# Audio tower on one core: the long filter's matrices in 128-column bands, and two VectorE steps in another place

## The chip, the core and the metric

One Trainium2 chip, one of its cores. The metric is the time of one execution on the device in microseconds; "before" is the median of three runs. The profile is of one further execution.

## What is computed

The input is 32 sequences of 750 x 256 in float32. Of each, every second token of three 256-token segments is kept: 3 blocks of 128 tokens. The reference then is, cut to what matters:

```python
h = tok(x)                                 # softmax attention inside each block of 128
h = h + attn(layernorm(h))                 # below
h = h + ffn(layernorm(h))                  # 6 experts, the best 2 of each token weighted
# attn:
q, k, v = (silu(causal_dwconv(x @ W, w4)) for each of Wq, Wk, Wv)
beta = sigmoid(x @ Wb)
delta_out = delta_rule(q, k, v, beta)      # chunked, carries a state over the blocks
fir_short = causal_dwconv(v, fir_short_w)  # 3 taps
fir_long  = causal_dwconv(v, fir_long_w)   # 63 taps, own taps for each of 256 channels
w = softmax(mlp([x, stats of the four branches]) / temp)   # per head
o = w0 * fir_short + w1 * fir_long + w2 * delta_out + w3 * v
return (rmsnorm(o) * o_norm_w) @ Wo
```

The long filter is done as matrix products. For a channel with taps f, a matrix with T[p, j] = f[62 - (j - p)] (non-zero only for j - p from 0 to 62) takes the 128 tokens p of a block to outputs j of the same block (j < 128) and of the next one (j from 128 to 189). Rows p below 64 end at column 125, so they reach no output of the next block.

## The kernel before

The kernel has three stages, each a block of hand-written queues: what an engine does, and when, is the order of the code of that engine, and engines meet through semaphores only. SyncE (SP) issues most DMAs, ScalarE (ACT) the stores of the filtered rows, GpSimd (POOL) the loads and stores of the triangular systems.

**First stage** (`first_phase`): for each of 32 sequences the block attention, the norm, the projections, the short convolutions and what the delta rule needs; results are packed and stored to DRAM (`packa`, `packb`, `systems`), and v is kept on chip in `v_all` (128 tokens x 256 channels x 96 columns, a column a block of a sequence). Beside this SP writes the matrices of the long filter: for each row p of 128 one DMA (`expand`, line 349) copies 190 consecutive taps of each of 256 channels, shifted by p, from `taps` to `toeplitz` in DRAM. 4 rows go out with each sequence.

**Middle stage** (`second_phase`): the long filter on TensorE, in 32 groups (`it`) of 8 channels (`CG`). SP loads a group's matrices into one of four buffers `toep` (`NT = 4`, line 1040); the load of group `it` waits until group `it - 4` has been multiplied (`fl_ready`). For every 4 channels (half a group) TensorE does four main products (line 1073: 128 rows, 128 output tokens, 96 columns) and four spill products (line 1077: what runs over into the next block; 62 output tokens, 64 columns), all float32, each of which the trace shows as two passes. ScalarE copies each half group from PSUM (line 1089). Ten, then three times six passes of a wide product with the identity (`dense`, line 1057) stand at the head of the stage and ahead of groups 8, 16 and 24; their results are not used. VectorE meanwhile solves triangular systems, SP loads the last stage's weights between the bands.

**Last stage** (`third_phase`): a loop of 35 steps, each of which works on four sequences at once: `n = i` in the delta rule, `it = i - 1` in the gate and the mixture, `e = i - 2` in the output projection, the routing and experts 0 to 2, `f = i - 3` in experts 2 to 5. The names that matter here, all on VectorE unless said:

- `delta_out(n, s, b)` (line 1983): scales block b's output from bank 1 into `DL`. TensorE's `q_state(b + 1)` (line 1543) writes bank 1 next and waits for it (`d_ready`).
- `remainder(n, b)` (line 1966): `R` = `VB` - bank 0. TensorE's `updates(b)` (line 1555) reads `R` (`r_copied`).
- `state(n, b)` (lines 1975, 1977): the state from bank 2 into `S`.
- `gate_weights(it)` (lines 2009 to 2013): the four branch weights `WT`. GpSimd's `weigh_fir` and `weigh_v` (lines 2273, 2278) wait for them, and multiply 768 columns each.
- `routing_weights(e)` (lines 2095, 2097, 2099, 2101): the two kept routes' weights `we`; 2095 and 2101 multiply two SBUF tensors of 18 columns.
- `weigh(it, s, r)` (lines 2019, 2022): `DL` or the filtered rows times `WT`, 768 columns.
- `add_expert(e, k, b)` (line 2111): adds expert k's output of block b from PSUM. TensorE's `expert_out` (line 1672) of the same bank waits for it (`acc_done`); `expert_out(e, 0, 2)` waits for `add_expert(f, 5, 2)`.
- `mix_add` (line 2028): sums the branches.

## Time and profile before

| | us |
|---|---|
| median of 3 runs | 2378.38 (2372.26 to 2381.79) |
| the profiled execution | 2393.8 |
| its span, first to last instruction | 2392.1 |
| first stage, to about | 656 |
| middle stage | 656 to 812 |
| last stage | 817 to 2392 |
| TensorE busy | 2251.9 (94%) |
| VectorE busy | 1852.8 (77%) |
| ScalarE busy | 1290.8 (54%) |
| GpSimd busy | 555.5 (23%) |
| moved by DMA | 334.44 MB |

A busy TensorE is not one at its peak: the ends of its instructions are modelled and its clock can be granted at 1.0 (2.4 GHz) or 0.5 (1.2 GHz) of full speed, which the profile gives for every stretch. A DMA share is the mean busy share of 16 DMA engines; it can read a little above 1.

### The profile page before, as it was taken

What the parts mean: (1) busy time and instruction counts of PE and PEld (TensorE: products, weight loads), DVE (VectorE), ACT (ScalarE), POOL (GpSimd) and SP (SyncE); (2) the same over time, 40 slices, a digit from 0 to 9 for tenths busy, and PEclk for the clock granted to TensorE, in tenths of its full rate; (3) what the DMA queues carried; (4) which work ended last, traced back from release to release, by engine and by line L of the source; (5) the groups of instructions that cost most, each with busy time, mean ns of one, the idle gap of its engine ahead of it and who ended that gap; (6) DMA issues with size and microseconds to landing.
All of it is one profiled execution on the core that took longest, in us unless ns stands there. A gap on an engine that the chain in (4) does not pass through costs nothing.

```text
span 2392.1 us, 53303 instructions
## 1 busy us (share of the span) xinstructions
PE 2251.9 (94%) x20796; PEld 1635.1 (68%) x20796; DVE 1852.8 (77%) x5111; ACT 1290.8 (54%) x2632; POOL 555.5 (23%) x413
## 2 busy tenths in 40 slices
PE   5999999999799779999999999999999999999997
PEld 4666666666587666777677767776776677767765
DVE  4999999999868367677778777777777667767765
ACT  4888888888624334544454455445544544454452
POOL 1444444444400011121112111111111121112111
PEclk9999999999958879999999999999999999999999
DMA  3776777777778912233224222322233224222300
GB/s 98 231 245 229 229 241 245 236 238 236 247 241 314 378 60 71 71 108 96 78 70 139 91 77 71 125 81 74 70 132 105 71 70 133 77 71 76 125 21 21
DMA packets 224297, 334.44 MB, mean 140 GB/s; under 512 B 113870, under 2 KB 190766, under 8 KB 215342
## 3 DMA queue, kind: packets, MB, share of 16 engines
q1 hardware_dynamic: 219726, 309.01, 39.1%
q10 hardware_dynamic: 2304, 12.58, 1.3%
q0 software_dynamic: 2016, 9.44, 1.0%
q8 instruction: 165, 2.70, 0.5%
q14 instruction: 86, 0.70, 0.1%
HBM read 191.66 MB, written 164.23 MB: 149 GB/s over the span
## 4 chain that ended last, share of the span: by engine, by line
PE 49%; DVE 7%; ACT 6%; issue 4%; POOL 0%; DVEq 0%
PE bank L1662 7%; PE bank L1672 7%; PE bank L1595 6%; PE bank L1475 4%; PE bank L1555 4%; PE bank L1632 4%; PE bank L1571 2%; PE bank L1507 2%; PE bank L1543 2%; ACT L1808 2%; ACT L1803 2%; DVE v_all L2111 1%; PE bank L1503 1%; PE bank L1485 1%; DVE DL L2019 1%
## 5 line engine op out<-in xcount | busy, mean ns | idle before, releaser
L2111 DVE SCALAR_TENSOR_TENSOR v_all<-bank,we,v_all 128x256 f32<-128x256 f32 x576 | 264.9, 476 | 219.3 <-PE bank L1672 214.3
L739 DVE SCALAR_TENSOR_TENSOR Y<-bank,convw,Y 128x383 f32<-128x383 f32 (+2 forms) x576 | 330.6, 602 | 3.2 <-ACT Y L627 2.9
L1672 PE MATMUL bank<-w2e,HE 128*128 128x256 f32 x1152 | 327.9, 395 | 2.4 <-DVE v_all L2111 2.3
L1662 PE MATMUL bank<-v_all,w1e 128*128 128x384 f32 x768 | 289.6, 500 | 2.4 <-ACT HE L1808 2.3
L445 PE MATMUL bank<-pb,wqkv 128*128 128x384 f32 x768 | 282.4, 491 | 1.8 <-DVE Y L739 1.8
L1672 PEld LDWEIGHTS bank<-w2e,HE 128*128 128x128 f32 x1152 | 198.0, 191 | 55.3 <-issue 19.3
L1808 ACT ACTIVATE HE<-bank 128x384 f32<-128x384 f32 x192 | 94.1, 490 | 248.9 <-PE bank L1662 248.2
L1595 PE MATMUL bank<-v_all,w1g 128*128 128x384 f32 x512 | 193.4, 500 | 2.0
L1662 PEld LDWEIGHTS bank<-v_all,w1e 128*128 128x128 f32 x768 | 134.5, 191 | 75.9 <-issue 19.8
L445 PEld LDWEIGHTS bank<-pb,wqkv 128*128 128x128 f32 x768 | 132.1, 191 | 61.1 <-DVE Y L739 8.3
L1786 ACT ACTIVATE first_stage<-bank 32x384 f32<-32x384 f32 (+1 forms) x192 | 92.2, 480 | 135.7 <-PE bank L1583 119.2
L2273 POOL TENSOR_TENSOR v_all<-v_all,WT 128x768 f32<-128x768 f32 x32 | 48.6, 1518 | 418.0 <-DVE WT L2013 418.0
L627 ACT ACTIVATE Y<-bank,convw 128x384 f32<-128x384 f32 x192 | 114.0, 594 | 46.6 <-PE bank L445 46.6
L2283 POOL TENSOR_TENSOR m<-m,minus_half_q 128x12 f32<-128x12 f32 x32 | 72.6, 2268 | 282.2 <-DVE m L2034 282.2
L1475 PE MATMUL bank<-v_all 64*128 64x256 f32 x768 | 114.4, 418 | 12.7 <-PEq L1030 5.9
L1595 PEld LDWEIGHTS bank<-v_all,w1g 128*128 128x128 f32 x512 | 89.7, 190 | 51.9 <-ACT v_all L1803 14.0
L1786 ACT ACTIVATE W<-bank 128x256 f32<-128x256 f32 x96 | 36.9, 384 | 150.2 <-PE bank L1555 150.2
L2267 POOL TENSOR_TENSOR VB<-v_all 128x768 f32<-128x768 f32 x32 | 47.1, 1472 | 279.8 <-DVE v_all L2062 212.5
L1950 DVE BATCH_NORM_STATS2 ST<-v_all 128x6 f32<-128x128 f32 x384 | 102.3, 282 | 7.7 <-DMA first_stage<-fl 7.7
L2259 POOL TENSOR_TENSOR b<-b,minus_half_q 128x3 f32<-128x3 f32 x32 | 27.1, 848 | 335.0 <-DVE b L2058 335.0
L1475 PEld LDWEIGHTS bank<-v_all 64*128 64x128 f32 x768 | 69.2, 194 | 50.0 <-issue 36.6
L1939 DVE TENSOR_TENSOR v_all<-bank,upper 128x256 f32<-128x256 f32 x192 | 74.4, 416 | 34.6 <-PE bank L1475 34.6
(217 smaller groups left out, 5199.1 us busy)
## 6 DMA issues: line engine op xcount, KB each, us to landing
packa<-pa SPq DMA_DIRECT2D x32, 1932.0 KB, 6.2
v_all<-packa SPq DMA_DIRECT2D x32, 1932.0 KB, 8.1
packb<-pb SPq DMA_DIRECT2D x32, 768.0 KB, 6.1
v_all<-packb SPq DMA_DIRECT2D x32, 768.0 KB, 10.8
toeplitz<-taps SPq DMA_DIRECT2D x128, 190.0 KB, 5.3
toep<-toeplitz SPq DMA_DIRECT2D x32, 760.0 KB, 7.6
packb<-fsk SPq DMA_DIRECT2D x32, 384.0 KB, 2.7
first_stage<-fl SPq DMA_DIRECT2D x32, 384.0 KB, 8.7
```

Of the source, the lines that this page charges most:

```text
L445: mm = pe.matmul(proj_bank[j][:, 0:T], wqkv[:, a, j * P:(j + 1) * P], xnT[:, a, :], start=(a == 0), stop=(a == HALF - 1), skip_group_check ...
L627: act.activation(Y[:, j, :], proj_bank[j][:, 0:T], ACT.Copy, scale=convw[:, j, CK - 1:CK])\
L739: dve.scalar_tensor_tensor(out=Y[:, j, lag:T], in0=proj_bank[j][:, 0:T - lag], scalar=convw[:, j, CK - 1 - lag:CK - lag], in1=Y[:, j, lag: ...
L1475: mm = pe.matmul(bank[odd][:, hh * 2 * P:(hh + 1) * 2 * P], kT[rows, hh, pair * P:(pair + 1) * P], qkb[rows, :, hh, pair * P:(pair + 1) * ...
L1555: mm = pe.matmul(bank[2][:, (h + 1 - wide) * DH:(h + 1) * DH], UF[s][:, even_heads_first(b, h), :], right.unsqueeze(1).broadcast_to([P, wi ...
L1595: pe.matmul(mlp_bank[m][:, 0:T], w1g[:, a, m * P:(m + 1) * P], chans(pb[s], PX)[:, a, :], start=(a == 0), stop=False, skip_group_check=True)
L1662: mm = pe.matmul(bank[6][:, 0:T], w1e[:, a, k, :], YT[s][:, a, :], start=(a == 0), stop=(a == HALF - 1))
L1672: pe.matmul(expert_bank(b), HE[k % 2][:, b * P:(b + 1) * P], w2e[:, k, :], start=True, stop=True)\
L1786: return act.activation(dst, src, ACT.Copy)
L1808: act.activation(HE[k % 2][:, :], bank[6][:, 0:T], ACT.Gelu_apprx_tanh).then_inc(he_ready.sem, 1)
L1950: return dve.bn_stats(ST[:, r, j, :], values[:, 2 * j:2 * j + 2, :].rearrange("p m d -> p d m"))
L2111: dve.scalar_tensor_tensor(out=HA[s][:, b, :], in0=expert_bank(b), scalar=we[s][:, b, k:k + 1], in1=HA[s][:, b, :], op0=ALU.mult, op1=ALU. ...
```

## The change

1. `toeplitz` in DRAM has 128 columns for each row and channel (`BAND`) where it had 190. A row p from 64 up starts 64 columns later, so that its band holds columns 64 to 191 of the matrix.
2. A buffer `toep` has 192 columns a channel (`TW`). A group is loaded by two DMAs: rows 0 to 63 into columns 0 to 127, rows 64 to 127 into columns 64 to 191. The pieces are 512 bytes.
3. The corners that no load writes and the main product reads (rows from 64, columns 0 to 63) are cleared once by VectorE, which TensorE waits for once (`toep_cleared`).
4. The spill product reads rows 64 to 127 only, and has 64 output tokens.
5. In the last stage `delta_out(n, 0)` stands ahead of `routing_weights`, `remainder(n, 1)` ahead of `weigh(it, 2)`, and `remainder(n, 2)` ahead of `add_expert(e, 1, 0)` and `(e, 1, 1)`. Nothing else moves there.

```diff
-TW = P + FL - 1
+BAND = P
+TW = DH + BAND
...
-                        sp.dma_start(dram["toeplitz"][p], dram["taps"][:, bass.ds(P - 1 - p, TW)]).then_inc(expanded, 16)
+                        sp.dma_start(dram["toeplitz"][p], dram["taps"][:, bass.ds(P - 1 - p + p // DH * DH, BAND)])\
+                            .then_inc(expanded, 16)
...
-                    sp.dma_start(toep[it % NT][:, :, :], dram["toeplitz"][:, it * CG:(it + 1) * CG, :])\
-                        .then_inc(toep_loaded[it % NT].sem, 16)
+                    for k in range(P // DH):
+                        rows = slice(k * DH, (k + 1) * DH)
+                        sp.dma_start(toep[it % NT][rows, :, k * DH:k * DH + BAND],
+                                     dram["toeplitz"][rows, it * CG:(it + 1) * CG, :]).then_inc(toep_loaded[it % NT].sem, 16)
...
                 dense(5)
+                pe.wait_ge(tail["toep_cleared"], NT)
...
-                                mm = pe.matmul(acc[0:TW - P, o + NB:o + BLK * NB], toep[s][:, ch, P:],
-                                               v_all[:, it * CG + ch, 0:(BLK - 1) * NB],
+                                mm = pe.matmul(acc[0:TW - P, o + NB:o + BLK * NB], toep[s][DH:P, ch, P:],
+                                               v_all[DH:P, it * CG + ch, 0:(BLK - 1) * NB],
...
+                for s in range(NT):
+                    dve.memset(toep[s][DH:P, :, 0:DH], 0.0).then_inc(tail["toep_cleared"], 1)
...
                         gate_weights(it)
+                    if 0 <= n < NB:
+                        delta_out(n, n % 2, 0)
                     if 0 <= e < NB:
                         routing_weights(e, e % 2)
+                    if 0 <= n < NB:
+                        remainder(n, 1)
                     if 0 <= it < NB:
                         weigh(it, it % 2, 2)
-                    if 0 <= n < NB:
-                        delta_out(n, n % 2, 0)
-                        remainder(n, 1)
...
+                    if 0 <= n < NB:
+                        remainder(n, 2)
                     if 0 <= e < NB:
                         add_expert(e, 1, 0)
                         add_expert(e, 1, 1)
                     if 0 <= n < NB:
-                        remainder(n, 2)
                         delta_out(n, n % 2, 1)
```

Where the instructions stand. First VectorE in the middle of a step of the last stage, from the end of `gate_weights` on; before:

```order
L2013 TENSOR_TENSOR WT<-WT,m 128x48
L2095 TENSOR_TENSOR e<-e 128x18
L2097 TENSOR_REDUCE g<-e 128x3
L2099 RECIPROCAL g<-g 128x3
L2101 TENSOR_TENSOR we<-e,g 128x18
L2019 TENSOR_TENSOR DL<-DL,WT 128x768
L1983 TENSOR_TENSOR DL<-bank,v_all 128x256
L1966 TENSOR_TENSOR R<-VB,bank 128x256
L2111 SCALAR_TENSOR_TENSOR v_all<-bank,we,v_all 128x256
```

And changed (the lines of this part of the file are 8 further down):

```order
L2021 TENSOR_TENSOR WT<-WT,m 128x48
L1991 TENSOR_TENSOR DL<-bank,v_all 128x256
L2103 TENSOR_TENSOR e<-e 128x18
L2105 TENSOR_REDUCE g<-e 128x3
L2107 RECIPROCAL g<-g 128x3
L2109 TENSOR_TENSOR we<-e,g 128x18
L1974 TENSOR_TENSOR R<-VB,bank 128x256
L2027 TENSOR_TENSOR DL<-DL,WT 128x768
L2119 SCALAR_TENSOR_TENSOR v_all<-bank,we,v_all 128x256
```

`delta_out` (1983, now 1991) passed five instructions, `remainder` (1966, now 1974) one.

Second, VectorE later in the same step, around `remainder(n, 2)`; before:

```order
L2028 TENSOR_TENSOR DL<-DL,v_all 128x768 x2
L2111 SCALAR_TENSOR_TENSOR v_all<-bank,we,v_all 128x256 x2
L1966 TENSOR_TENSOR R<-VB,bank 128x256
L1983 TENSOR_TENSOR DL<-bank,v_all 128x256
L2111 SCALAR_TENSOR_TENSOR v_all<-bank,we,v_all 128x256
```

And changed:

```order
L2036 TENSOR_TENSOR DL<-DL,v_all 128x768 x2
L1974 TENSOR_TENSOR R<-VB,bank 128x256
L2119 SCALAR_TENSOR_TENSOR v_all<-bank,we,v_all 128x256 x2
L1991 TENSOR_TENSOR DL<-bank,v_all 128x256
L2119 SCALAR_TENSOR_TENSOR v_all<-bank,we,v_all 128x256
```

`remainder` passed two expert additions.

Third, SP's queue at the head of the middle stage (`toep` loads, and weights of the last stage between them); before:

```order
L1040 DMA toep<-toeplitz 128x1520 x6
L974 DMA itemp<-in_L_attn_gate_log_temp_dram 128x4
L975 DMA rclip<-in_L_ffn_routing_temp_dram 128x1
L1040 DMA toep<-toeplitz 128x1520
L971 DMA onw<-in_L_attn_o_norm_w_dram 64x1 x2
```

And changed:

```order
L1045 DMA toep<-toeplitz 64x8x128 x12
L977 DMA itemp<-in_L_attn_gate_log_temp_dram 128x4
L978 DMA rclip<-in_L_ffn_routing_temp_dram 128x1
L1045 DMA toep<-toeplitz 64x8x128 x2
L974 DMA onw<-in_L_attn_o_norm_w_dram 64x1 x2
```

Each load of 128 rows of 1520 elements became two of 64 rows of 8 pieces of 128 elements; the order is the same.

## Rows read from the trace of the kernel before

**Rows 1.** Windows by stage: us, busy us (instructions) per engine, clock, DMA share, GB/s

```profile
60.00:640.00 580.00, 542.80 (x6413) 389.15 (x6411) 573.48 (x1505) 478.55 (x1051) 263.46 (x213) 1.00 0.73 236
664.00:812.00 148.00, 141.91 (x1042) 123.24 (x1042) 110.42 (x169) 57.85 (x72) 6.14 (x12) 0.78 0.83 304
900.00:2300.00 1400.00, 1374.97 (x11941) 984.67 (x11940) 1027.28 (x3044) 666.10 (x1332) 244.06 (x147) 1.00 0.27 89
```

**Rows 2.** Waits of TensorE, 900 to 2300 us: total us, times, longest

```profile
PE bank L1543 <- DVE DL L1983: 12.4, 29, 0.5
PE bank L1555 <- DVE R L1966: 8.9, 29, 0.3
```

**Rows 3.** Windows of 5 us in the middle stage, columns as in rows 1

```profile
675.00:680.00 5.00, 5.00 (x29) 4.54 (x29) 4.66 (x11) 1.18 (x2) 0.00 (x0) 0.50 0.51 156
...
735.00:740.00 5.00, 0.78 (x4) 0.78 (x4) 4.80 (x6) 0.25 (x1) 0.00 (x0) 0.73 1.02 420
...
785.00:790.00 5.00, 5.00 (x50) 4.52 (x49) 4.83 (x6) 1.73 (x3) 0.00 (x0) 1.00 1.03 423
```

**Rows 4.** Timeline, TensorE, middle stage: start us, us, instruction, [idle before]

```profile
663.87 1.13 PE L1073 MATMUL bank<-v_all,toep 128*128 128x96 f32 x8 [2.19 <-DMA toep<-toeplitz]
...
677.41 2.02 PE L1073 MATMUL bank<-v_all,toep 128*128 128x96 f32 x8
...
680.40 2.02 PE L1073 MATMUL bank<-v_all,toep 128*128 128x96 f32 x8
...
720.91 1.13 PE L1073 MATMUL bank<-v_all,toep 128*128 128x96 f32 x8
...
722.57 1.13 PE L1073 MATMUL bank<-v_all,toep 128*128 128x96 f32 x8
```

**Rows 5.** Waits, 655 to 830 us; the load of line 1040 issued at 724.3 us

```profile
PE bank L1073 <- DMA toep<-toeplitz: 8.1, 4, 4.8
...
DMA to landing us min/median/max: 14.9/14.9/14.9
```

**Rows 6.** Windows with inputs (1 KB), solved systems (128 B), filtered rows (768 B)

```profile
63.00:64.00 1.00, 1.00 (x5) 0.52 (x4) 1.00 (x3) 1.00 (x4) 0.00 (x0) 1.00 0.93 372
...
830.50:831.00 0.50, 0.50 (x39) 0.50 (x36) 0.00 (x0) 0.00 (x0) 0.00 (x0) 0.50 1.23 151
...
834.00:834.50 0.50, 0.50 (x7) 0.50 (x6) 0.00 (x0) 0.00 (x0) 0.00 (x0) 0.50 1.14 376
```

**Rows 7.** Timeline, one step of the last stage: start us, us, instruction, [idle before]

```profile
1541.28 0.17 DVE L2095 TENSOR_TENSOR e<-e 128x18 f32<-128x18 f32 x1
1541.45 1.50 POOL L2273 TENSOR_TENSOR v_all<-v_all,WT 128x768 f32<-128x768 f32 x1 [12.52 <-DVE WT L2013]
...
1541.91 1.07 DVE L2101 TENSOR_TENSOR we<-e,g 128x18 f32<-128x18 f32 x1
1542.90 0.95 DVE L2019 TENSOR_TENSOR DL<-DL,WT 128x768 f32<-128x768 f32 x1
1542.90 1.03 PE L1672 MATMUL bank<-w2e,HE 128*128 128x256 f32 x4
...
1543.88 0.42 DVE L1983 TENSOR_TENSOR DL<-bank,v_all 128x256 f32<-128x256 f32 x1
...
1544.36 0.71 PE L1543 MATMUL bank<-first_stage,v_all 128*128 128x128 f32 x4 [0.43 <-DVE DL L1983]
1544.55 0.48 DVE L2111 SCALAR_TENSOR_TENSOR v_all<-bank,we,v_all 128x256 f32<-128x256 f32 x1
...
1544.90 1.00 PE L1555 MATMUL bank<-R,first_stage 128*128 128x128 f32 x8
...
1545.74 0.65 PE L1672 MATMUL bank<-w2e,HE 128*128 128x256 f32 x2
...
1550.60 1.46 PE L1662 MATMUL bank<-v_all,w1e 128*128 128x384 f32 x4
...
1552.36 0.82 PE L1555 MATMUL bank<-R,first_stage 128*128 128x128 f32 x5 [0.30 <-DVE R L1966]
```

More of the change, by code:

```diff
@@ L101, in audio_tower @@
             "taps": nc.dram_tensor("taps", [D, 512], F32, kind="Internal").ap(),
-            "toeplitz": nc.dram_tensor("toeplitz", [P, D, TW], F32, kind="Internal").ap(),
+            "toeplitz": nc.dram_tensor("toeplitz", [P, D, BAND], F32, kind="Internal").ap(),
         }
@@ L942, in kept_semaphores @@
                   late_stored=sem("late_stored"), fl_stored=[sem(f"fl_stored{g}") for g in range(NH)],
-                  toep_loaded=[Signal(sem(f"toep_loaded{s}"), 16, primed=0) for s in range(NT)],
+                  toep_cleared=sem("toep_cleared"),
+                  toep_loaded=[Signal(sem(f"toep_loaded{s}"), 16 * P // DH, primed=0) for s in range(NT)],
                   fl_ready=Signal(sem("fl_ready"), 2, primed=0), fl_copied=Signal(sem("fl_copied"), 2, primed=0))
```

## The prediction

> **What bounds the kernel now.** I read first the busy time by stage [rows 1], to see which engine each stage has no slack on. In the first stage VectorE is busy 573.48 of 580 us and the DMA engines 0.73 of the time: VectorE bounds it. In the last stage TensorE is busy 1374.97 of 1400 us and VectorE 1027.28: TensorE bounds it, and what it can lose or win is its waits. The middle stage has TensorE busy 141.91 of 148 us, but at a mean granted clock of 0.78, so "busy" hides a slow clock.
>
> Then the waits of TensorE in the last stage [rows 2]: two places carry nearly all of its idle time, line 1543 behind `delta_out` (12.4 us, 29 times) and line 1555 behind `remainder` (8.9 us, 29 times). These are the two steps that the change moves.
>
> Then the middle stage in slices [rows 3] and as a timeline [rows 4]. At 675 to 680 us TensorE is 100% busy at clock 0.50 (1.2 GHz) with the DMA engines 0.51 busy; at 785 to 790 it is as busy at 1.00 (2.4 GHz) with the DMA engines 1.03 busy. In the timeline half a group (4 channels) takes 2.99 us at the low clock (677.41 to 680.40) and 1.66 us at the high one (720.91 to 722.57), so a group costs 5.99 or 3.31 us. The clock is low after two idle stretches: 2.19 us before the first band lands at 663.87 and the starved slice 735 to 740 (TensorE busy 0.78 of 5 us). The load issued at 724.3 landed 14.9 us later, and the longest of TensorE's waits for a load was 4.8 us, of 8.1 in all [rows 5]; with four buffers and 3.31 us a group, a load has 13.2 us. So this stage is bound by DMA landings and by what the clock does behind them.
>
> **The change, part by part.**
>
> *Building the bands (first stage).* 128 DMAs write 128 columns for each of 256 channels, where they wrote 190. Nothing computes with them in this stage and VectorE is what bounds it [rows 1], so I cost it at nothing. The cover is large: a third fewer bytes cannot make it later.
>
> *Clearing the corners.* Four VectorE memsets of 64 rows x 512 elements stand at the head of the middle stage, in front of VectorE's wait for the first stage's stores. TensorE waits for them once, behind ten dense matmuls, after which it sits idle 2.19 us for the first band anyway [rows 4]. Nothing, unless the four took longer than those matmuls and that idle together; the 768-column multiply takes 0.95 us [rows 7], so four of 512 columns are under 4.
>
> *The second matmul of each channel.* It reads 64 rows and 64 columns for 128 rows and 62. In half a group eight main passes take 1.13 us of 1.66 [rows 4], so eight spill passes take about 0.6 us; two columns more in 62 is 3% of that at the most, 0.02 us x 64 halves = 1.2 us. I take nothing for it.
>
> *The loads.* A group was one DMA of 128 rows of 6080 bytes; now it is two DMAs of 64 rows, each row 8 pieces of 512 bytes (1024 pieces, 64 for each of 16 DMA engines, against 8 rows each). What an engine needs for a piece has to come from neighbours. At 785 to 790 us the DMA engines move 423 GB/s at a share of 1.03 [rows 3], nearly all in rows of 4 KB and more: 25.7 GB/s an engine, so 6080 bytes take 237 ns and a group 8 x 237 = 1.90 us. No row has 512-byte pieces into SBUF. Pieces of 1 KB (the inputs) move 372 GB/s at 0.93, 41 ns each; of 768 bytes (the filtered rows) 376 at 1.14, 37 ns; of 128 bytes (the solved systems) 151 at 1.23, 17 ns [rows 6]. The straight line from 128 to 768 bytes gives 29 ns at 512, so 64 x 29 = 1.86 us a group. The bounds are 20 ns (512 bytes at 25.7 GB/s), 1.28 us, and 37 ns (a piece costs what a 768-byte one does), 2.37 us. I take 29 ns, which lies between two measured neighbours: **a third fewer bytes, but the same DMA time**. So the late landing near 739 us stays late, the two low-clock stretches stay, and the stage gives 0 us, with -0.6 to +0.5 us a group as its bounds.
>
> *The first moved step (last stage).* Rows 7 show one step. `delta_out(0)` (line 1983) ends at 1544.30 and line 1543 starts at 1544.36; TensorE's line 1672 before it (4 passes, from 1542.90, 0.217 us apart) would have let it start at 1543.77, so this wait costs 0.59 us. The order now is `delta_out(0)`, four small routing operations, `remainder(1)`, the 0.95 us `weigh`. `delta_out(0)` reads PSUM and ends at about 1541.75: line 1543 starts at 1543.77. But look at GpSimd. Its multiply of 1.50 us begins at 1541.45, and line 2101, a VectorE multiply of two SBUF tensors with 18 columns, takes 1.07 us and ends as that multiply ends; its sister line 2095, issued 0.17 us before GpSimd starts, takes 0.17. Behind `delta_out(0)` line 2095 is issued at about 1541.65, inside GpSimd's multiply, and waits until 1542.95; GpSimd's second multiply, of the same size, then begins, and line 2101, ready at 1543.6, waits until about 1544.5. `remainder(1)` ends at about 1544.85, line 1555 starts at 1544.90 as before, and the 0.59 us is given back. Worse, `weigh` and then the expert addition end at 1546.1 where it was 1545.03; line 1672, which starts at 1545.74 and needs it, now starts 0.42 us late.
>
> The Trainium skill (SBUF — State Buffer, Who interferes with whom) states this as a rule: a VectorE instruction with two SBUF inputs and a GpSimd instruction that reads SBUF exclude each other, and the second to issue blocks for the whole of the first. The trace agrees at line 2101 (1.07 us for 0.17). Without such an exclusion the first move would be worth its 0.59 us.
>
> *The second moved step.* `remainder(2)` comes ahead of two expert additions. Line 1662 (4 passes of 0.486 us from 1550.60, 0.325 apart) would let line 1555 start at 1551.89; it starts at 1552.36, 0.47 us late. The two additions that now stand behind it take 0.48 us each, more than the wait, so the wait goes. They end 0.4 us later; line 1672 that needs them stands behind eight passes of line 1555 and four of 1543. Late next is `delta_out(1)`, by my count 0.1 us ahead of its reader.
>
> **Sum.** A step: +0.42 - 0.47 = -0.05 us, x 30 steps = -1.5 us; middle 0; first 0. The profiled execution took 2393.8 us (span 2392.1), 15 us above the median of 2378.38, so I subtract from the median: **2377 us**. About 0.5%, 12 us, is what a measurement of this kernel tells from no change.
>
> **Rivals.**
>
> 1. *The exclusion does not bite* (GpSimd starts later, or line 2095 slips in front). Then both waits go, 0.59 + 0.47 = 1.06 us x 30 = -32 us: 2346 us. For it: both waits are real [rows 2]. Against it: line 2101.
>
> 2. *The bands land sooner.* At 20 ns a piece, the five groups queued before 739 us land 3 us sooner; the 4.8 us wait shrinks to under 2, shorter than the 2.19 us after which the clock fell, and two groups at 3.31 instead of 5.99 us give 5 more. If the first band also comes in time for TensorE to stay at 2.4 GHz, the eight groups before the first dense block between groups give 8 x 2.68 = 21 us. So -10 to -30 us: 2358 us. Against it: 768-byte pieces are already slower per byte than 1 KB ones [rows 6].
>
> 3. *Slower: the half-height loads starve TensorE.* If 64 rows take in only half the full rate (411/2 = 205 GB/s), each half of a group (262 KB) takes 1.28 us, a group 2.56, +0.66 us. It decides wherever the DMA engines have no slack: five groups before 739 us (+3 us) and the last 16 groups (785 to 790 us: share 1.03), +11 us; where a wait then drops the clock, each group costs 2.68 us more. +14 us, up to +35: 2392 us. No row shows a 64-row load of any size, so nothing here excludes it. The Trainium skill (SBUF — State Buffer, Door 1) says that partitions 0 to 63 reach 8 of 16 DMA ports and that two loads on the two halves serialize. By its 218 GB/s a group would take 2.4 us (an estimate from that page). Against it: stores on ScalarE's queue fill the gaps.
>
> 4. *The late expert addition costs more than the second move returns*: 0.42 us a step without the 0.47 is +13 us, 2391 us.
>
> **How the numbers follow.** Forecast (within 12 us) 0.41; rival 1 0.14, rival 2 0.17; rival 3 0.21, rival 4 0.07. So faster 0.31, same 0.41, slower 0.28. The forecast's own range is 2366 to 2388. Rival 1 at its full size sets the low end, 2346; rival 3 with some clock loss sets the high end, 2400; its +35 us is left out.
>
> **What would show it.** Right: the granted clock still 0.50 for the first eight groups, with a DMA share of about 0.5; a load near 724 us landing after some 15 us; the first routing multiply (line 2103 of the changed kernel) taking about 1.3 us and the last (2109) about 1.0, with no wait at line 1543 for b = 1 and a new wait of about 0.4 us at line 1672 behind the expert addition; steps as long as now. Wrong: both routing multiplies at 0.17 us (rival 1), the middle stage shorter than 140 us (rival 2), or TensorE waits on the band loads well over 8.1 us and a DMA share near 1 with fewer GB/s (rival 3).

## The result, and the profile after

| | before | changed |
|---|---|---|
| median, us | 2377.81 (4 runs) | 2403.91 (4 runs) |
| lowest to highest | 2372.26 to 2381.79 | 2400.04 to 2414.30 |
| ratio | | 1.012 (1.0094 to 1.0146) |
| the profiled execution | 2393.8 | 2400.7 |

The change makes the kernel 1.2% slower, +26 us, where 2377 was forecast. The two profiled executions lie only 7 us apart: the profile of before is of one of its longer executions (2393.8 us against a median of 2377.81), as the experiments below show.

The stages first, windows of the changed kernel (columns as in rows 1):

```profile
60.00:640.00 580.00, 543.12 (x6450) 389.40 (x6449) 573.64 (x1506) 478.44 (x1052) 264.21 (x214) 1.00 0.65 223
664.00:812.00 148.00, 139.94 (x936) 120.49 (x935) 110.41 (x169) 52.25 (x65) 5.94 (x11) 0.71 0.92 225
900.00:2300.00 1400.00, 1376.34 (x11905) 997.73 (x11905) 1057.96 (x3053) 664.78 (x1330) 223.40 (x148) 1.00 0.28 91
```

Against [rows 1]: the first stage is as it was, with less DMA (share 0.65 for 0.73). The middle stage has 936 matmul passes in the same 148 us for 1042, at a clock of 0.71 for 0.78; the DMA engines are busier (0.92 for 0.83) and move less (225 GB/s for 304). That is the reading that decides: the DMA engines are nearly full through the whole stage and do less.

The head of the middle stage, 5 us windows of the changed kernel; beside them [rows 3] and, at 660 to 670, 403 and 413 GB/s before:

```profile
660.00:665.00 5.00, 2.47 (x15) 1.41 (x14) 0.55 (x12) 0.00 (x0) 1.84 (x3) 1.00 1.03 206
665.00:670.00 5.00, 5.00 (x33) 4.47 (x31) 0.00 (x0) 1.64 (x2) 0.00 (x0) 0.58 1.11 253
670.00:675.00 5.00, 4.07 (x25) 3.60 (x24) 0.00 (x0) 1.64 (x2) 0.00 (x0) 0.50 1.12 257
675.00:680.00 5.00, 4.71 (x24) 4.42 (x24) 3.93 (x11) 0.83 (x1) 0.00 (x0) 0.50 1.23 199
```

A share over 1 with 199 to 257 GB/s: all engines are occupied and move 49 to 62% of what they did at the head before (403 and 413 GB/s). From 670 us on TensorE is not full even at 1.2 GHz. Its waits in this stage, 655 to 830 us:

```profile
PE bank L1079 <- DMA toep<-toeplitz: 10.6, 6, 4.7
```

That is 10.6 us for 8.1 in [rows 5], little beside the 12 us by which the two profiles differ in this stage; a list of waits doesn't show the time that a busy TensorE spends at 1.2 GHz. Whether the clock is the cause or only follows the late loads, this profile can't tell; the run with fourteen dense passes below can.

How long one packet takes is read from the DMA summary of 660 to 680 us (20 us of 16 engines, 320 us in all), the load queue's row; first before, then changed:

```profile
q1 hardware_dynamic: 1359, 4.69, 61.6%
```
```profile
q1 hardware_dynamic: 6053, 2.98, 83.2%
```

Changed: 0.832 x 320 / 6053 = 44 ns a packet, nearly all of them the 512-byte pieces. A group is 0.524 MB: 266.2 us / 2.98 MB x 0.524 / 16 = 2.93 us of all engines. Before it was 197.1 / 4.69 x 0.778 / 16 = 2.04 us. (The share is the packets' time as the profile counts it, so these figures serve to compare kernels in the same window and no more.) The prediction had 29 ns and 1.86 us.

The last stage, one step of the changed kernel, timeline (columns as in rows 7):

```profile
1552.79 0.42 DVE L1991 TENSOR_TENSOR DL<-bank,v_all 128x256 f32<-128x256 f32 x1
1552.84 1.50 POOL L2283 TENSOR_TENSOR v_all<-v_all,WT 128x768 f32<-128x768 f32 x1 [12.50 <-DVE WT L2021]
...
1553.13 1.24 DVE L2103 TENSOR_TENSOR e<-e 128x18 f32<-128x18 f32 x1
...
1554.30 1.50 POOL L2288 TENSOR_TENSOR v_all<-v_all,WT 128x768 f32<-128x768 f32 x1
...
1554.82 1.00 DVE L2109 TENSOR_TENSOR we<-e,g 128x18 f32<-128x18 f32 x1
1555.16 0.61 PE L1551 MATMUL bank<-first_stage,v_all 128*128 128x128 f32 x4
1555.75 0.41 DVE L1974 TENSOR_TENSOR R<-VB,bank 128x256 f32<-128x256 f32 x1
...
1556.21 1.10 PE L1563 MATMUL bank<-R,first_stage 128*128 128x128 f32 x8 [0.44 <-DVE R L1974]
1556.95 0.47 DVE L2119 SCALAR_TENSOR_TENSOR v_all<-bank,we,v_all 128x256 f32<-128x256 f32 x1
...
1557.47 0.70 PE L1680 MATMUL bank<-w2e,HE 128*128 128x256 f32 x2 [0.16 <-DVE v_all L2119]
...
1563.67 1.00 PE L1563 MATMUL bank<-R,first_stage 128*128 128x128 f32 x8
```

This is the predicted step nearly to the number: 2103 held until GpSimd's first multiply is done (1.24 us), 2109 until its second is (1.00), line 1551 without a wait, `remainder(1)` late again (0.44 us at line 1563), a new wait at line 1680, and the second `remainder` in time. TensorE's waits, 900 to 2300 us:

```profile
PE bank L1563 <- DVE R L1974: 14.7, 30, 1.8
PE bank L1680 <- DVE v_all L2119: 4.5, 28, 0.2
```

19.2 us for the 21.3 of [rows 2].

### The profile page after: what moved, and what is told of

It reads as the page before. It is cut to its first block, busy times and chain, and to the rows that moved or that the text cites. A ratio compares the mean times of both kernels' runs of the same rounds, so it can differ in the third digit from the quotient of the medians.

```text
span 2399.0 us, 53340 instructions
## 1 busy us (share of the span) xinstructions
PE 2257.6 (94%) x20796; PEld 1650.2 (69%) x20796; DVE 1880.5 (78%) x5115; ACT 1289.0 (54%) x2632; POOL 531.4 (22%) x413
## 4 chain that ended last, share of the span: by engine, by line
PE 57%; ACT 6%; DVE 4%; DMA 3%; issue 2%; SPq 0%; POOL 0%; ACTq 0%; DVEq 0%
PE bank L1670 10%; PE bank L1680 9%; PE bank L1603 6%; PE bank L1483 4%; PE bank L1640 4%; PE bank L1579 3%; PE bank L1079 3%; PE bank L1563 2%; PE bank L1515 2%; DMA toep<-toeplitz 2%; ACT L1816 2%; PE bank L1083 2%; ACT L1811 2%; DVE DL L2027 1%; PE bank L1610 1%
## 5 line engine op out<-in xcount | busy, mean ns | idle before, releaser
L1670 PEld LDWEIGHTS bank<-v_all,w1e 128*128 128x128 f32 x768 | 133.9, 190 | 76.3 <-issue 19.2
L1079 PE MATMUL bank<-v_all,toep 128*128 128x96 f32 x512 | 93.1, 339 | 10.6 <-DMA toep<-toeplitz 10.6
```

What stands on the lines that cost most here:

```text
L1079: pe.matmul(acc[:, o:o + BLK * NB], toep[s][:, ch, 0:P], v_all[:, it * CG + ch, :], start=(k == 0), stop=False, skip_group_check=True)
L1670: mm = pe.matmul(bank[6][:, 0:T], w1e[:, a, k, :], YT[s][:, a, :], start=(a == 0), stop=(a == HALF - 1))
```

## The experiments

Each is a change to the kernel before or to the changed one; ratios are to the kernel before. First the change in its two parts.

**The moved steps alone.**

```diff
+                    if 0 <= n < NB:
+                        delta_out(n, n % 2, 0)
...
+                        remainder(n, 1)
...
+                        remainder(n, 2)
```

> The kernel before with only the two moved steps of the last stage; full bands of 190 columns as before. The changed kernel's trace shows a step of 47.38 to 47.54 us with the routing multiplies held at 1.24 and 1.00 us. Theory A (the loss of about 26 us is all in the bands, the moves give a little): about -0.16 us a step, -5 us, ratio 0.998, routing multiplies at about 1.24 and 1.00 us, no wait behind line 1983 at line 1543 for block 1. Theory B (the moves do the harm, through the late expert addition, +0.42 us a step): +13 us, ratio 1.005. Theory C (whatever lies between the two): moves and bands add up, so this run and the one with the bands alone give the changed kernel's +26 us in their sum.

Measured: 2370.94 us, ratio 0.997 (0.9946 to 0.9994): -5 us by the medians, -7 by the ratio. The routing multiplies take 1.23 and 1.00 us, as expected. So theory A holds: the moves give a little and the loss isn't theirs.

**The bands alone** (the changed kernel with its last stage put back):

```diff
-                    if 0 <= n < NB:
-                        delta_out(n, n % 2, 0)
                     if 0 <= e < NB:
                         routing_weights(e, e % 2)
```

> The changed kernel with the last stage's order put back; only the bands differ from the kernel before. Theory A (the bands do the harm): +25 to +31 us against the kernel before, ratio 1.011 to 1.013; in the middle stage long waits of TensorE for the bands' loads, a DMA share over 1 with 200 to 260 GB/s around 660 to 680 us, a mean clock near 0.7. Theory B (the moves do it): within 5 us of the kernel before, as the forecast of 29 ns a piece had it. Theory D (part of the loss is how the clock falls in a given execution): the times of this kernel scatter over 10 us or more, and those runs that are long have the lower mean clock.

Measured: 2411.87 us, ratio 1.0129 (1.0093 to 1.0165): theory A. The medians are 36 us apart, the ratio makes it +31. The parts add up to within 5 us: by the ratios -7 and +31 us against +28 for both, by the medians -5 and +36 against +26. The middle stage, from the first dense pass to the end of the last spill product, takes 168.5 us here, 168.2 in the changed kernel and 136.8 with the moves alone, whose loads are those of before. So **the loss is some 31 us of the middle stage**, give or take what this stage varies by itself (see the part on the prediction).

Now what of a band load costs this: its height or its pieces.

**Half the height, full rows** (on the kernel before):

```diff
+                    for k in range(P // DH):
+                        rows = slice(k * DH, (k + 1) * DH)
+                        sp.dma_start(toep[it % NT][rows, :, :], dram["toeplitz"][rows, it * CG:(it + 1) * CG, :])
```

> The kernel before (its order in the last stage, full rows of 6080 bytes), but each group loaded by two DMAs of 64 rows instead of one of 128. It isolates the height. Theory P (pieces: a piece of 512 bytes costs an engine about 41 ns, the height costs nothing): no change against the kernel before, within 5 us, windows at 665 to 670 us and 785 to 790 us still over 400 GB/s at a share near 1.0. Theory H (height: 64 rows take in only about half the rate, 205 GB/s): 3.8 us a group instead of 1.9, so the 32 groups take 122 us of DMA time where the stage has 148 with other loads beside: +40 us or more, and windows near 200 GB/s.

Measured: 2415.24 us, ratio 1.0147 (1.0108 to 1.0186), +38 us by the medians, with no shorter piece and no byte less. Theory H, at the lower edge of its +40. The windows, whose counterparts before moved 413 GB/s at a share of 1.01 and 285 at 0.71:

```profile
665.00:670.00 5.00, 5.00 (x32) 4.54 (x31) 0.00 (x0) 0.83 (x1) 0.00 (x0) 0.54 1.00 232
670.00:675.00 5.00, 5.00 (x27) 4.55 (x25) 0.00 (x0) 1.65 (x2) 0.00 (x0) 0.50 1.03 269
```

**Full height in two DMAs** (the control: 4 of 8 channels each):

```diff
+                    for k in range(2):
+                        ch = slice(k * CG // 2, (k + 1) * CG // 2)
```

> The control of the half-height run: the kernel before, a group again in two DMAs, but each of all 128 rows and 4 of the 8 channels (rows of 3040 bytes). Theory H (the height): as the kernel before within 5 us, ratio 0.998 to 1.002, windows of over 400 GB/s at full share. The rival (what the half-height run lost by is the second DMA of each group, its issue and its start): near that run's 2415 us, +20 us or more.

Measured: 2381.89 us, ratio 0.9993 (0.9966 to 1.002), and 389 to 411 GB/s from 665 to 675 us. With rows of this length (3040 bytes) the second DMA is free; the height is not.

**One load of 128 rows in 512-byte pieces** (on the run with the bands alone):

```diff
-                    for k in range(P // DH):
...
+                    sp.dma_start(toep[it % NT][:, :, DH:DH + BAND], dram["toeplitz"][:, it * CG:(it + 1) * CG, :])
```

> The run with the bands alone, but a group is one DMA of 128 rows in 512-byte pieces, all into columns 64 to 191 of the buffer, with columns 0 to 63 cleared. It leaves out the right position of the bands of rows 0 to 63, so the long filter is not computed rightly; the instructions and bytes are the same. It isolates the pieces. Theory P: the same as with the bands alone, +30 to +36 us against the kernel before, windows of 200 to 260 GB/s at a share over 1. Theory H: 512 KB a group at the full rate, 1.3 to 1.9 us a group: as the kernel before or up to 20 us faster, no windows under 300 GB/s with a full share.

Measured: 2386.30 us, ratio 1.0031 (1.0002 to 1.006). Its profile is of its longest execution (2407.68 us), so only the packets are read from it. Its load queue at 660 to 680 us:

```profile
q1 hardware_dynamic: 6274, 2.99, 57.1%
```

0.571 x 320 / 6274 = 29.1 ns a packet, the 29 ns of the prediction, and 2.0 us a group, what the group cost before. So the pieces were priced rightly. Theory P, that a piece costs 41 ns at any height, falls; H holds as to the loads, but not its gain: +9 us by the medians is left (+7 by the ratio).

**The same band as one row of 4096 bytes:**

```diff
-        toep = [sb(f"toep{s}", [P, CG, TW]) for s in range(NT)]
+        toep = [sb(f"toep{s}", [P, CG, BAND]) for s in range(NT)]
```

> As the run before it, but the buffer holds 128 columns a channel and nothing else, so one DMA writes each row of it as 4096 bytes in one run; the spill product reads columns 64 to 127 of rows 64 to 127. It leaves out the right position of the bands and the cleared corners, so the long filter is not computed rightly. A group is 128 pieces of 4096 bytes: at 25.7 GB/s an engine 159 ns each, 1.28 us a group. Theory P: the third fewer bytes now count: 10 to 25 us faster than the kernel before, full share only with over 380 GB/s, TensorE's waits for the loads under 4 us. Theory H: no different from the run with one load of 512-byte pieces.

Measured: 2369.82 us, ratio 0.9951 (0.9925 to 0.9977): -7 us by the medians and -12 by the ratio. Neither theory has it whole: H expected no difference from the run before (2386.30 us), and it is 16 us less; P expected 10 to 25 us under the kernel before, which it meets by the ratio only. So the 512-byte pieces do cost, at full height too: the same bytes in long rows are 16 us faster. TensorE's waits for the loads fell to 0.3 us. The products end at 779.0 us, after 121.2 us, 16 less than with the moves alone; but the last stage can't start then. TensorE's first wait of the last stage, and the windows of its end:

```profile
PE bank L1478 <- PEq L1033: 12.9, 1, 12.9
```
```profile
780.00:785.00 5.00, 0.00 (x0) 0.00 (x0) 4.83 (x6) 0.00 (x0) 0.00 (x0) 0.77 1.02 419
785.00:790.00 5.00, 0.00 (x0) 0.00 (x0) 4.61 (x6) 0.00 (x0) 0.00 (x0) 0.50 1.01 421
790.00:795.00 5.00, 2.08 (x8) 1.26 (x8) 1.01 (x3) 0.58 (x2) 1.47 (x1) 0.50 1.06 432
```

VectorE is full with its triangular systems until 789.8 us while TensorE stands still, and line 1478 starts at 791.88. That wait was 5.9 us before, so by this reading 7 of the 16 us are given to VectorE, the next bound of this stage. The reads-first run below, whose products end at 783.6 us, has the same wait of 12.9 us.

**Rows spread over all partitions.** As the half-height run, but by even and odd rows:

```diff
-                        rows = slice(k * DH, (k + 1) * DH)
+                        rows = slice(k, P, 2)
```

> The half-height run (full rows of 6080 bytes, two DMAs of 64 rows for a group), but one DMA has the even rows and the other the odd rows, so that each is spread over all 128 partitions. Theory R (the region: rows in one half of the partitions take in less): as the kernel before, within 5 us of 2380 us, windows of over 400 GB/s at full share. Theory N (the number of rows: a DMA of 64 rows is slow wherever its rows lie): as the half-height run, 2410 to 2420 us, windows of 200 to 270 GB/s at full share.

Measured: 2376.65 us, ratio 1.0011 (0.9979 to 1.0043), against 1.0147 for the same 64 rows a DMA in one half. Its windows:

```profile
665.00:670.00 5.00, 5.00 (x50) 4.49 (x48) 0.00 (x0) 2.49 (x3) 0.00 (x0) 1.00 1.00 386
670.00:675.00 5.00, 5.00 (x50) 4.50 (x49) 0.00 (x0) 2.50 (x3) 0.00 (x0) 1.00 0.97 376
```

Three of its twelve executions took 2397 to 2401 us, like the longer ones of the kernel before. Theory R, though the windows are a little under the 400 GB/s that it expected: not the number of rows, but **that they are 64 neighbours**. The Trainium skill (SBUF — State Buffer, Door 1) gives 8 of 16 ports and 218 GB/s to partitions 0 to 63, where rows with a stride of 2 would reach all 16. This run and the half-height run agree; the half-height windows are above 218 (232 and 269 GB/s), with some 70 GB/s of another queue's loads among them (1.40 MB from 660 to 680 us). In every run here neighbouring rows on the chip are neighbouring rows in DRAM too; none moves one without the other, so that the cause lies on the chip's side is the Trainium skill's account and is not shown by itself.

**The same with 512-byte pieces** (on the one load):

```diff
+                        rows = slice(k, P, 2)
+                        sp.dma_start(toep[it % NT][rows, :, DH:DH + BAND], dram["toeplitz"][rows, it * CG:(it + 1) * CG, :])
```

> The run with one load of 512-byte pieces (2386 us), but in two DMAs, of the even and of the odd rows. Like that run it leaves out the right position of the bands of rows 0 to 63. Theory R: as that run, 2383 to 2390 us, and a packet of the load queue at 29 ns at 660 to 680 us. Theory N: as the run with the bands alone, 2405 to 2415 us, 40 ns and more a packet.

Measured: 2399.20 us (2384.38 to 2403.91), ratio 1.01 (1.0068 to 1.0133). By time it is outside both theories, 13 us above the one load and 13 under the bands alone. By the packet, R: 0.544 x 320 / 6161 = 28.3 ns, not 44.

```profile
q1 hardware_dynamic: 6161, 2.94, 54.4%
```

The profiled execution took 2384.38 us at a mean clock of 0.974, the five others 2398 to 2404 at 0.966 to 0.969. So the long ones have the lower clock, but no profile shows one of them, and why two such loads cost 13 us more than one stays open. For 512-byte pieces that the neighbours are the cause is shown by the packets and by the one load, not by this run's time: of the +31 us of the bands alone, by the ratios, spread rows gave back 7 and the one load 23.

**Both halves at once**, the upper one on ScalarE's queue:

```diff
+                def load_upper(it):
+                    act.dma_start(toep[it % NT][DH:P, :, DH:DH + BAND],
+                                  dram["toeplitz"][DH:P, it * CG:(it + 1) * CG, :]).then_inc(toep_loaded[it % NT].sem, 16)
```

> The run with the bands alone, with the loads of rows 64 to 127 on ScalarE's queue instead of SyncE's, so that both halves of a buffer can be written at once: the first four at the head of the stage, each later one behind ScalarE's copies of the group that frees its buffer. Pieces and heights are those of the changed kernel. Theory H (one half of the rows takes only part of the rate, and the two halves stood one behind the other in one queue): most of the loss comes back, 2380 to 2392 us, as the one load of 512-byte pieces had, with windows of 300 GB/s and more. The rival (a 64-row DMA is slow by itself, whatever runs beside it, or the pieces are): as with the bands alone, 2405 to 2415 us.

Measured: 2404.36 us, ratio 1.009 (1.0065 to 1.0115), a miss: 8 us of 36 came back. With both queues loading, the head of the stage moved no more than with one (214 and 246 GB/s in the same windows with the bands alone):

```profile
660.00:665.00 5.00, 3.70 (x8) 1.36 (x6) 0.42 (x12) 0.00 (x0) 0.27 (x1) 0.84 1.03 185
665.00:670.00 5.00, 3.37 (x32) 3.01 (x32) 0.13 (x1) 1.42 (x2) 1.57 (x3) 1.00 1.23 201
```

So "half the partitions, half the rate, two halves together the full rate" is not what this run shows. A load of 64 neighbouring rows stays slow at the head of the stage even beside one of the other half. Rival 3 of the prediction had said so, that two loads on the two halves serialize; the expectation's theory H had it the other way. Why it is so stays open: the rival in the last expectation of the next group puts it down to two engines sharing a region of the partitions, and no run looks at that by itself.

**4 KB between the rows in DRAM.** A row of the matrices is 131072 bytes since the change, where it was 194560. Three of the kernels above were run again with a longer row:

```diff
-            "toeplitz": nc.dram_tensor("toeplitz", [P, D, BAND], F32, kind="Internal").ap(),
+            "toeplitz": nc.dram_tensor("toeplitz", [P, D + 8, BAND], F32, kind="Internal").ap(),
```

The changed kernel:

> The changed kernel with 4 KB more between the rows of the matrices in DRAM (264 instead of 256 channels in the tensor, 8 unused), so that the pitch is 135168 bytes instead of 131072. Theory H (the 64 neighbouring partitions alone): no change, 2400 to 2407 us. Theory Q (the power-of-two pitch takes part, since the reads of all 16 engines step by it): 5 to 20 us faster, and a packet at 660 to 680 us well under 44 ns. The Trainium skill (DMA Engines, HBM row pitch at large powers of two, in its list of limits) reports lower rates at pitches of 512 KB and more and calls the mechanism an inference; no run here has tested a pitch by itself.

The one load of 512-byte pieces:

> The run with one load of 128 rows in 512-byte pieces (2386 us), with the same 4 KB between the rows in DRAM; it also leaves out the right position of the bands of rows 0 to 63. Theory Q: 2370 to 2378 us, under 27 ns a packet. The rival (what that run lost is the clock's fall, not the loads): as that run, 2384 to 2390 us, 29 ns a packet.

Both halves at once:

> The run with both halves at once from two queues (2404 us), with the same 4 KB between the rows in DRAM. Theory Q: at the head of the stage 300 GB/s and more instead of 185 to 201, and 2380 to 2390 us. The rival (two engines share one region of the partitions in each half, on both queues at once): as that run, 2400 to 2408 us, near 200 GB/s.

Measured: 2405.46 (2403.91 without), 2385.98 (2386.30) and 2402.52 us (2404.36), and 186 to 204 GB/s with both halves at once. Theory Q falls in all three. The second of them has its profile in a usual execution (2388.17 us), and its head suggests where the one load's +9 us come from:

```profile
656.06 5.81 PE L1060 MATMUL bank<-v_all,ident 128*128 128x480 f32 x10 [1.82 <-PEq L298]
663.96 1.10 PE L1077 MATMUL bank<-v_all,toep 128*128 128x96 f32 x8 [2.09 <-DMA toep<-toeplitz]
664.99 0.68 PE L1081 MATMUL bank<-v_all,toep 64*64 64x64 f32 x8
665.60 1.68 PE L1077 MATMUL bank<-v_all,toep 128*128 128x96 f32 x8
```

Behind 2.09 us of idle time TensorE falls to 1.2 GHz within the second half group (1.68 us for 1.13), as in the profile of before; this stage takes 151.3 us, 4.5 less than there. All twelve executions have a mean clock of 0.976 or less, where most of the kernel before have 0.976 or more. So the loads seem to win a little and the clock at the head to lose more; no run held the clock there with this load, so this is argued, not shown.

**The spill product alone** (on the kernel before):

```diff
-                                mm = pe.matmul(acc[0:TW - P, o + NB:o + BLK * NB], toep[s][:, ch, P:],
+                                mm = pe.matmul(acc[0:TW - P, o + NB:o + BLK * NB], toep[s][DH:P, ch, P:],
```

> The kernel before with its full loads, but the spill product reads rows 64 to 127 only (62 output tokens, as before). It tests the second matmul of the change by itself, and whether it explains that the one load of 512-byte pieces was 10 us slower than the kernel before though its DMA time a group was less. By the forecast: no change, within 3 us. The rival: a product of 64 rows lets TensorE's clock fall sooner or runs longer: +5 to +12 us, with a lower mean clock.

Measured: 2378.70 us, ratio 0.9984 (0.9958 to 1.001). It costs nothing, and does not explain the one load's +9 us.

Then the clock. **Fourteen dense passes for ten at the head of the changed kernel's middle stage:**

```diff
-                dense(5)
+                dense(7)
```

> The changed kernel with dense(7) instead of dense(5) at the head of the middle stage: 14 dense passes instead of 10, about 7.9 us at 2.4 GHz, so that TensorE idles 1 us instead of 2.5 us for the first band. In the profiles TensorE kept 2.4 GHz through an idle stretch of 0.59, 1.20 or 1.26 us there and fell to 1.2 GHz behind 2.19, 2.53 and 2.60 us. Theory K (about half of the 26 us is that the first band now lands too late for the clock, in every execution instead of some): 12 to 20 us faster than the changed kernel, ratio to the kernel before 1.003 to 1.006, the groups up to 680 us at 1.66 us a half. The rival: the later starved stretches drop the clock anyway and the stage ends when the DMAs end: within 5 us of the changed kernel, 1.010 to 1.012.

Measured: 2406.14 us, ratio 1.011 (1.0077 to 1.0143): nothing. The rival holds. The clock did stay at first, and the time went to waiting instead:

```profile
665.00:670.00 5.00, 4.62 (x42) 3.99 (x41) 0.00 (x0) 1.66 (x2) 0.35 (x1) 1.00 1.15 235
670.00:675.00 5.00, 2.33 (x25) 2.03 (x24) 0.00 (x0) 1.64 (x2) 0.00 (x0) 1.00 1.09 291
675.00:680.00 5.00, 4.61 (x24) 4.33 (x24) 2.13 (x7) 0.82 (x1) 0.00 (x0) 0.54 1.18 195
```

At 2.4 GHz TensorE runs ahead of the bands, idles 2.67 of 5 us at 670, and is at 1.2 GHz by 675. In the changed kernel the loads set the pace of the first groups, whatever the clock is; the low clock at the head does not make this loss.

Last, whether the reading of the last stage holds when it is used. **Reads of PSUM first, routing where it was:**

```diff
                     if 0 <= e < NB:
                         routing_weights(e, e % 2)
-                    if 0 <= it < NB:
-                        weigh(it, it % 2, 2)
                     if 0 <= n < NB:
                         delta_out(n, n % 2, 0)
                         remainder(n, 1)
                     if 0 <= f < NB:
                         add_expert(f, 5, 2)
+                    if 0 <= it < NB:
+                        weigh(it, it % 2, 2)
...
+                        remainder(n, 2)
```

> The kernel before with another order of VectorE's middle of a step: routing weights, delta_out(0), remainder(1), add_expert(f, 5, 2), then weigh(2); and the second move (remainder(2) ahead of the two expert additions). The routing multiplies stand where they stood, delta_out(0) and remainder(1) pass only the 0.95 us multiply. Theory A (the exclusion gave the first move back because delta_out pushed the routing multiply into GpSimd's): both waits go, 0.59 + 0.47 us a step, and line 1672 has its expert addition earlier than before: -25 to -32 us, ratio 0.987 to 0.990; the first routing multiply at 0.17 us. The rival: weigh(2) ends 0.9 us later and what follows it (mix_add, remainder(2), or the clearing of bank 0 and 1) becomes late: under -10 us.

Measured: **2341.95 us, ratio 0.9851 (0.981 to 0.9891), -34 us**: it beats both kernels. TensorE is busy 1394.08 of 1400 us of the last stage. From its first instruction there (796.51 us) to the end (2339.1) it takes 1542.6 us, where the profile of before has 1574.4 (817.74 to 2392.1): 32 us less, so the gain does lie in this stage. The routing multiplies, and for comparison those of the moves alone (groups of instructions, 900 to 2300 us; busy, mean ns):

```profile
L2101 DVE TENSOR_TENSOR we<-e,g 128x18 f32<-128x18 f32 x31 | 33.0, 1064 | 1.1
...
L2095 DVE TENSOR_TENSOR e<-e 128x18 f32<-128x18 f32 x31 | 5.3, 171 | 0.0
```
```profile
L2095 DVE TENSOR_TENSOR e<-e 128x18 f32<-128x18 f32 x30 | 37.0, 1234 | 0.0
...
L2101 DVE TENSOR_TENSOR we<-e,g 128x18 f32<-128x18 f32 x30 | 30.1, 1003 | 1.0
```

**Routing ahead of everything:**

```diff
                         keep_best(e)
+                        routing_weights(e, e % 2)
```

> The kernel before with routing_weights right behind keep_best (ahead of state and gate_weights, so before GpSimd's multiplies start), then state, gate_weights, delta_out(0), remainder(1), add_expert(f, 5, 2), weigh(2); and the second move. Theory A (the exclusion is what holds the routing multiplies): all routing multiplies at about 0.17 us, 1.07 us of VectorE's time in a step won beside both waits, -25 to -35 us, ratio 0.985 to 0.990; no more than the run before it if TensorE is full by then. The rival: four small operations more ahead of state and gate_weights make TensorE wait for the state (0.4 us a step): nothing gained over the run before it, or -15 us only.

Measured: 2343.14 us, ratio 0.9844 (0.9809 to 0.9879), no more than the run before. Both routing multiplies are short now, and the exclusion has gone to the next VectorE instructions with two SBUF tensors:

```profile
L2022 DVE TENSOR_TENSOR v_all<-first_stage,WT 128x768 f32<-128x768 f32 x31 | 69.6, 2246 | 0.0
...
L2019 DVE TENSOR_TENSOR DL<-DL,WT 128x768 f32<-128x768 f32 x31 | 41.3, 1331 | 0.0
...
L2095 DVE TENSOR_TENSOR e<-e 128x18 f32<-128x18 f32 x31 | 5.5, 179 | 5.7 <-ACT e L1862 5.6
L2101 DVE TENSOR_TENSOR we<-e,g 128x18 f32<-128x18 f32 x31 | 5.5, 178 | 1.1
```

Against the run before, line 2022 takes 2.25 us for 0.95 and line 2019 1.33 for 1.18: 1.5 us more, where 0.9 us was saved at line 2101. TensorE's waits in this stage have neither, so it costs nothing, and wins nothing.

**The reads-first order and `dense(7)`** for `dense(5)`, loads as before:

> The order of the reads-first run (2342 us) with dense(7) for dense(5) at the head of the middle stage, loads as in the kernel before. In 10 of 23 executions of the kernel before the time was 2389 us or more or the mean clock 0.975 or less, others were at 2372 to 2381; the profiles show that the difference is the first eight groups at 1.2 instead of 2.4 GHz, behind 2.19 us of idle TensorE. Theory K: 14 passes fill the time to the first band, all executions are like the good ones: 2336 to 2343 us and none over 2350. The rival: the longer chain ends after the first band has landed and only delays it: 2343 to 2346 us.

Measured: 2343.22 us (2338.88 to 2348.60), ratio 0.9834 (0.98 to 0.9868). All six are under 2350, where one of six of the reads-first order was at 2360.83; the median is no lower. So theory K may hold for the long executions, though six are too few to show it; for the median its rival does. (The expectation counts 10 of 23 longer executions of the kernel before; the record has 7 of 23 at or over 2389 us, and the same 7 at a clock of 0.975 or less.)

## Why the prediction was wrong, step by step

- **The first stage, the corners, the spill product: nothing.** Right. The first stage has the same busy times, and the spill product alone gives 0.9984.
- **The loads: "a third fewer bytes, but the same DMA time", 29 ns a piece, 1.86 us a group.** This step failed, and the size of the range with it. The piece was right (29.1 and 28.3 ns where the rows are not 64 neighbours), but the load was priced as if only its pieces mattered. At half the height a packet took 44 ns, above my upper bound of 37, and a group 2.93 us instead of 2.00 with the same pieces in one load. It was **rival 3**, with the mechanism I gave it, at 0.21: it had +0.66 us a group and +14 us, up to +35. Measured are +0.93 us a group against one load of the same pieces, and +31 us in the middle stage. I let it count only for 21 of the 32 groups, where I saw no slack; but at a share of 0.92 through the stage the slack was gone everywhere, and 32 x 0.93 = 30 us (an estimate from these rows) is near what was measured. The +35 was the nearer end, and I had left it out of the range, which stopped at 2400; 2403.91 was measured. Of the signs, the clock of 0.50 came as forecast, but a load issued near 724 us landed after 8.9 us and not 15, and the share of 1.11 to 1.23 with fewer GB/s from 665 to 680 us was rival 3's.
- **The clock in the middle stage: stays as in the profile.** Wrong for the median, because the profile of before misled me. It is an execution in which the clock fell at the first band. In the profile of the moves alone, with the same loads, it did not:

```profile
658.60 7.05 PE L1057 MATMUL bank<-v_all,ident 128*128 128x480 f32 x10 [1.82 <-PEq L297]
666.91 1.13 PE L1073 MATMUL bank<-v_all,toep 128*128 128x96 f32 x8 [1.26 <-DMA toep<-toeplitz]
667.97 0.67 PE L1077 MATMUL bank<-v_all,toep 128*62 128x64 f32 x8
668.57 1.13 PE L1073 MATMUL bank<-v_all,toep 128*128 128x96 f32 x8
```

  The ten dense passes ran partly at 1.2 GHz there, took 7.05 us for 5.64, and left 1.26 us of idle time for 2.19; the groups behind ran at 2.4 GHz, and the middle stage took 136.8 us for 155.8. The five other profiles with ten dense passes and loads of before's bytes at the full rate are like this one at the head. Their middle stages took 136.5 to 140.7 us, but 126.1 in the reads-first run. Against them the changed kernel's 168.2 is a loss of 28 to 32 us, and of 42 in that one case; the timed ratio of the bands alone, +31 us, is the firmer number. Over all profiles TensorE kept 2.4 GHz behind idle stretches of 0.3 to 1.5 us at this place (nine) and fell at once or within two half groups behind 1.9 to 3.5 us (nine); one of 2.30 us was passed at 2.4 GHz. In the timed executions of the kernel before beside the experiments, 79 of 100 (one outlier aside) took 2371 to 2388 us and 21 took 2390 to 2402, with a mean clock of 0.975 or less. So the kernel before seems to have, in most executions, the fast head that I took for rival 2's prize. Against such an execution the change loses 31 us of middle stage, against the profile I worked from only 12, which is why its own profile looked nearly harmless.
- **The sum against the median.** I subtracted from the median, rightly, but with the stage lengths of an execution 15 us longer. I should have asked where those 15 us lie; that TensorE might stay at 2.4 GHz at the head stood in rival 2.
- **The first moved step: 0.59 us won and given back.** Right, mechanism and numbers: "about 1.3" and "about 1.0" for 1.24 and 1.00 us.
- **The new wait of 0.42 us at line 1680.** It is 0.16 us. `remainder(1)` was 0.44 us late itself and took the rest: line 1680 stands behind eight passes of line 1563.
- **The second moved step: its wait goes.** Right; no wait at the second line 1563. In all -0.05 us a step was forecast; the moves alone gave -5 us by the medians, -0.16 us a step. The sign is right, the size is three times the forecast. Rival 4 had no place.
- **Rival 1** was no rival to this order, but the reads-first run shows its 32 us to be real (-34 us, 32 of them in the last stage) once the routing multiplies are not pushed into GpSimd's.

What stays open: why two halves loaded at once are no faster at the head, why two loads of 512-byte pieces on spread rows cost 13 us more than one, and what decides in a given execution whether the clock falls. With ten dense passes these took 5.6 to 6.4 us in eight of the nine profiles in which it fell and 6.8 to 7.3 in all but one in which it stayed, so a faster start may make the longer gap; no run set that on purpose.

## To carry to other kernels

Price a DMA by the partitions it covers before its bytes: in 512-byte pieces a load in halves of 64 neighbouring rows took 1.5 times the DMA time of one spread over 128 partitions (2.93 for 2.00 us). When the profiled execution lies 15 us from the median, find where these lie before its stage lengths are used. And where GpSimd and VectorE exclude each other, put VectorE's PSUM reads into GpSimd's time and its two-tensor multiplies outside it; count the held instructions and who waits for them, since moving the hold elsewhere (2.25 us for 0.95) is free only off the path.

## What the runs showed of the hardware

- 64 neighbouring rows: 44 ns a 512-byte packet, and 199 to 269 GB/s at full share (changed kernel and half-height run, 665 to 680 us); 64 rows at stride 2 or 128 rows: 28 to 29 ns, and 376 to 413 GB/s in long rows. Two queues on the two halves at once: 185 to 204 GB/s in the first 10 us.
- GpSimd's multiply holds whichever VectorE multiply of two SBUF tensors comes next: 1.23 us for 0.17 at line 2095, 2.25 for 0.95 at line 2022.
- With the same loads the middle stage took 136.8 us in a profile in which TensorE kept 2.4 GHz over an idle stretch of 1.26 us, and 155.8 in one in which it lost it behind 2.19 us.
- A busy TensorE can stay at 1.2 GHz: in the profile of before it is busy without a gap from 670 to 710 us at a granted clock of 0.50, and comes back with the six dense passes ahead of group 8 (710.34 to 714.55 us): the clock is 0.76 from 712 to 715 us and 1.00 from 715 to 720.
